# The image sort of a four-stage convolution block: four rounds made one, its turn from columns to lines cut in halves

## What is computed

```python
x = x + dct(_gn(x))                    # L0: keeps two bands of a 56x56 DCT
x = x + similarity(_gn(x), 5x5)        # L1: 5x5 patches weighted by cosine similarity over the channels
x = x + gate(_gn(x))                   # L2: a gate per channel
x = x + attention(_gn(x), ...)         # L3
```

```python
xh = x[:, :16]                                   # the first half of the channels
idx_h = argsort(xh, axis=-2); xs = take(xh, idx_h)   # sort each column
idx_w = argsort(xs, axis=-1); xs = take(xs, idx_w)   # then each line
x = concatenate([xs, x[:, 16:]], axis=1)
qkv = fuse(dw3(q), dw5(q), dw7(q)) of q = conv1x1(x)  # five words q1, k1, q2, k2, v
idx = argsort(v over the 3136 pixels)            # the row sort, which carries the four other words
...                                              # attention on sorted words
# the results go back through the inverse of idx, then of idx_w and idx_h
```

## Time and profile before

| | us |
|---|---|
| median of 3 runs | 14788.44 |
| lowest and highest | 14781.02, 14789.07 |
| profiled execution | 14787.32 |
| its span | 14785.4 |
| VectorE busy in it | 13633.2 |
| from the end of VectorE's last round on images to its first instruction of the row sort | 865.1 |

### The profile page before, as it was taken

How to read it: one execution, slowest core, us unless ns; L and a number is a source line. 1 busy time by engine, 2 the same in 40 slices (tenths; PEclk the granted TensorE clock), 3 DMA queues, 4 the chain that set the end, 5 groups by cost and what they waited for, 6 DMA issues and landing times. The chain is left out here.

```text
span 14785.4 us, 119905 instructions
## 1 busy us (share of the span) xinstructions
PE 6701.6 (45%) x42108; PEld 2746.8 (19%) x42108; DVE 13633.2 (92%) x7545; ACT 7055.5 (48%) x6343; POOL 5873.1 (40%) x3844
## 2 busy tenths in 40 slices
PE   4888825760037327426625714814823014433310
PEld 3444401210012112112111212201211002111100
DVE  4888878999999999999999999999999999989978
ACT  0000023455565665565575565565566555444443
POOL 0000000366666666666666666666666630000000
PEclk9999967885568668768857857956966557666655
DMA  1555532100001001001001000100100011221232
GB/s 46 140 140 145 149 78 68 51 27 12 11 12 45 17 11 41 22 12 36 27 11 36 27 12 30 32 12 26 37 12 12 34 33 50 87 67 54 79 76 66
DMA packets 342572, 696.70 MB, mean 47 GB/s; under 512 B 71005, under 2 KB 275006, under 8 KB 331126
## 3 DMA queue, kind: packets, MB, share of 16 engines
q1 hardware_dynamic: 337398, 673.49, 16.7%
q10 hardware_dynamic: 4544, 15.26, 0.4%
HBM read 479.77 MB, written 208.74 MB: 47 GB/s over the span
## 5 line engine op out<-in xcount | busy, mean ns | idle before, releaser
L1194 DVE COPY_PREDICATED arena<-psum,arena 128x2048 f32<-128x2048 uint32 (+23 forms) x1280 | 3968.9, 3104 | 71.3 <-ACT psum L1154 70.5
L1201 DVE COPY_PREDICATED arena<-psum,arena 128x2048 f32<-128x2048 uint32 (+23 forms) x1280 | 3932.9, 3076 | 42.0
L1020 PE MATMUL psum<-arena,wt 128*32 128x448 f32 x31360 | 3210.1, 571 | 1217.2 <-DMA arena<-xpad 695.1
L1119 POOL TENSOR_TENSOR arena<-arena 128x512 int32<-128x512 int32 (+23 forms) x1280 | 2037.7, 1593 | 3124.3 <-DVE arena L1186 3121.8
L1105 POOL TENSOR_TENSOR arena<-arena 128x512 bf16<-128x512 f32 (+23 forms) x1280 | 1930.8, 1509 | 3031.1 <-SPq L270 2830.8
L1142 ACT ACTIVATE arena<-arena 128x2048 f32<-128x2048 f32 (+23 forms) x1280 | 3032.1, 2371 | 70.4 <-DVE arena L1201 38.1
L1162 ACT ACTIVATE masks<-psum 128x512 fp8e4<-128x512 f32 (+25 forms) x1256 | 917.5, 731 | 3555.5 <-DVE arena L1201 3554.5
L1111 POOL TENSOR_TENSOR arena<-arena 128x512 int32<-128x512 int32 (+23 forms) x1280 | 1960.6, 1533 | 0.0
L1020 PEld LDWEIGHTS psum<-arena,wt 128*32 128x32 f32 x31360 | 1045.5, 114 | 3384.4 <-issue 2311.6
L1410 PE MATMUL psum<-ident,arena 128*112 128x128 f32 x896 | 196.9, 384 | 2432.2 <-ACT arena L1329 1872.9
L1186 DVE TENSOR_TENSOR arena<-arena 128x512 f32<-128x512 f32 (+23 forms) x1280 | 1146.5, 898 | 98.4 <-POOL arena L1111 98.4
(11 more groups left out here) (132 smaller groups left out, 7635.3 us busy)
## 6 DMA issues: line engine op xcount, KB each, us to landing
arena<-xpad SPq DMA_DIRECT2D x896, 108.5 KB, 2.3
arena<-simd SPq DMA_DIRECT2D x416, 210.0 KB, 4.2
arena<-simd SPq DMA_DIRECT2D x416, 196.0 KB, 4.1
xpad<-arena SPq DMA_DIRECT2D x8, 1924.0 KB, 8.1
arena<-in_x SPq DMA_DIRECT2D x8, 1568.0 KB, 7.5
x3d<-arena SPq DMA_DIRECT2D x8, 1568.0 KB, 5.2
prodd<-arena SPq DMA_DIRECT2D x8, 1568.0 KB, 5.2
arena<-prodd SPq DMA_DIRECT2D x8, 1568.0 KB, 14.7
```

Of the source, the lines that this page charges most:

```text
L1020: last = nc.tensor.matmul(psum[C * b:C * b + C, n % C_BANKS, 0:CROWS * W], wt[:, g, C * w:C * w + C], cx[i % 2][b][:, y0:y0 + CROWS, x0:x0 ...
L1119: last = nc.gpsimd.tensor_tensor(hi, packed_view(stmp, here, piece, 1), lo, ALU.subtract)
L1194: last = nc.vector.copy_predicated(lo, wide_mask(q, k, piece, here), hi)
L1201: last = nc.vector.copy_predicated(hi, wide_mask(q, k, piece, here), packed_view(ptmp, here, piece, NP))
```

## The change

All four images are sorted in one round. The two buffers `bk` become four: `bp` and `bq` for the column stages, `br` and `bs` for the line stages. `bx`, `bp`, `bq` and `bs` lie where the words of tile 1 of the row sort will be, `br` and `bin_` above tile 0's, so the convolution can write tile 0 meanwhile.

- **Start.** The load of `bin_` for u = 0 is issued before SP's part of the last `a_` round; that of `bx` stays behind it.
- **Between images.** ScalarE copies `bin_` of image u + 1 into `bp` behind stage 23 of image u (`first`). VectorE goes from stage 41 of one image to stage 0 of the next; ScalarE turns `bs` back into `bx` then.
- **The turn.** Stage 20 is done on columns 0 to 27 and then 28 to 55. ScalarE turns the first half behind the first, the second behind the second. Stage 21 is done on lines 0 to 27 when the first half is there and on lines 28 to 55 when the second is.
- **Loads.** The eight loads of the next image stand one by one behind the mask stores of stages 6 to 13, no longer together behind that of stage 5.
- **Convolution of tile 0.** One pass over all seven chunks through u = 1 to 3. The row sort's first round no longer waits for the last store to `xpad`; ScalarE does so before it writes the words of tile 1 (`stored`), and SP at that round's end.

The diff, of the functions `b_scalar` and `b_vector` only the new text (the old stands above):

```diff
...
         b_in, b_out, b_mst = sem("b_in"), sem("b_out"), [sem(f"b_mst{i}") for i in range(4)]
+        b_first, b_mid = sem("b_first"), sem("b_mid")
         b_cp, b_mk, b_hi, b_xp = sem("b_cp"), sem("b_mk"), sem("b_hi"), sem("b_xp")
 
-        b_sems = [*b_mst, b_cp, b_mk, b_hi, b_xp]
+        b_sems = [*b_mst, b_in, b_first, b_mid, b_cp, b_mk, b_hi, b_xp]
         st = [0]
-        bin_ = take(st, XPN)
         bx = take(st, XPN)
+        bp, bq, bs = (take(st, N) for _ in range(3))
+        assert st[0] <= NWD * N
+        st = [2 * NWD * N]
+        br, bin_ = take(st, N), take(st, XPN)
+        assert st[0] <= B_END
         bini, bxi = (v[:, 0:WP * WP].rearrange("p (h w) -> p h w", w=WP)[:, R3:R3 + H, R3:R3 + W] for v in (bin_, bx))
-        bk = [take(st, N), take(st, N)]
+        HALF = H // 2
         SI = len(IMG_NET)
 
         def turned(v):
             return v.rearrange("p (h w) -> p w h", w=W)
 
-        def b_load(sp, u, dst, loaded):
-            for b in range(UB):
+        def b_load(sp, u, dst, loaded, images=range(UB)):
+            for b in images:
                 sp.dma_start(dst[CS * b:CS * b + CS, :], xpad_u[u, b, 0:CS]).then_inc(loaded, 16)
 
-        def b_begin(sp):
-
-            b_load(sp, 0, bin_, b_in)
-            b_load(sp, 0, bx, b_out)
-
-        def b_sync(sp, u, beside, more):
+        def b_sync(sp, conv):
             count = [0] * 4
-            for d in range(2):
-                for s, (at, _, n) in enumerate(IMG_NET):
-                    q = d * SI + s
+            for u in range(U):
+                for i in range(2 * SI):
+                    d, s = divmod(i, SI)
+                    at, _, n = IMG_NET[s]
+                    q = 2 * SI * u + i
                     sp.wait_ge(b_mk, q + 1)
-                    sp.dma_start(img_masks[2 * u + d, :, at * W:(at + n) * W], masks[:, q % 4, 0:n * W]).then_inc(b_mst[q % 4], 16)
+                    sp.dma_start(img_masks[2 * u + d, :, at * W:(at + n) * W],
+                                 masks[:, q % 4, 0:n * W]).then_inc(b_mst[q % 4], 16)
                     count[q % 4] += 1
-                    if q == 2:
-                        sp.wait_ge(b_out, 16 * UB)
-                    if q % 3 == 2:
-                        next(beside, None)
-                    if q == 5 and more is not None:
-                        sp.wait_ge(b_cp, 1)
-                        sp.sem_clear(b_in)
-                        b_load(sp, more, bin_, b_in)
-            sp.wait_ge(b_xp, 1)
-            sp.sem_clear(b_out)
-            for b in range(UB):
-                sp.dma_start(xpad_u[u, b, 0:CS], bx[CS * b:CS * b + CS, :]).then_inc(b_out, 16)
-            for _ in beside:
+                    if u == 1 and i == 2:
+                        sp.wait_ge(b_out, 16 * UB * 2)
+                    if u and i % 3 == 2:
+                        next(conv, None)
+                    if u + 1 < U and 6 <= i < 6 + UB:
+                        if i == 6:
+                            sp.wait_ge(b_first, u + 1)
+                        b_load(sp, u + 1, bin_, b_in, (i - 6,))
+                sp.wait_ge(b_xp, u + 1)
+                for b in range(UB):
+                    sp.dma_start(xpad_u[u, b, 0:CS], bx[CS * b:CS * b + CS, :]).then_inc(b_out, 16)
+            for _ in conv:
                 pass
             for i in range(4):
                 sp.wait_ge(b_mst[i], 16 * count[i])
-            if more is None:
-                sp.wait_ge(b_out, 16 * UB)
...
+        def b_bufs(d, s):
+            a, b = (bp, bq) if d == 0 else (br, bs)
+            return (a, b) if s % 2 == 0 else (b, a)
+
+        def b_copied(u, d):
+
+            return (2 * SI + 2) * u + (SI + 2) * d
+
+        def b_scalar(act, conv):
+
+            def first(u):
+                act.wait_ge(b_in, 16 * UB * (u + 1))
+                if u:
+                    act.wait_ge(b_hi, 2 * SI * (u - 1) + SI)
+                nc.scalar.activation(img3(bp), bini, ACT.Copy).then_inc(b_first, 1)
+
+            first(0)
+            for u in range(U):
+                for i in range(2 * SI):
+                    d, s = divmod(i, SI)
+                    q = 2 * SI * u + i
+                    if i == SI:
+                        for h in range(2):
+                            if h == 0:
+                                act.wait_ge(b_mid, u + 1)
+                                act.wait_ge(b_cp, b_copied(u, 0) + SI)
+                            else:
+                                act.wait_ge(b_hi, q)
+                            w = slice(HALF * h, HALF * h + HALF)
+                            nc.scalar.activation(img3(br)[:, w, :], turned(bq)[:, w, :], ACT.Copy).then_inc(b_cp, 1)
+                    act.wait_ge(b_cp, b_copied(u, d) + s)
+                    if i == 0:
+                        act.wait_ge(b_first, u + 1)
+                    if q:
                         act.wait_ge(b_hi, q)
+                    src, dst = b_bufs(d, s)
+                    runs = unpaired(IMG_NET[s][1], H)
+                    for lo, hi in runs:
                         ins = nc.scalar.activation(dst[:, W * lo:W * hi], src[:, W * lo:W * hi], ACT.Copy)
                     if runs:
                         ins.then_inc(b_cp, 1)
                     else:
                         act.sem_inc(b_cp, 1)
+                    if u and i % 3 == 2:
+                        next(conv, None)
+                    if i == SI + 2 and u + 1 < U:
+                        first(u + 1)
+                act.wait_ge(b_hi, 2 * SI * (u + 1))
+                act.wait_ge(b_cp, b_copied(u + 1, 0))
+                act.wait_ge(b_out, 16 * UB * (u + 1))
+                nc.scalar.activation(bxi, turned(bs), ACT.Copy).then_inc(b_xp, 1)
+            for _ in conv:
                 pass
 
         def b_vector(dve):
+
+            def exchange(rows, src, dst, mask, part, marked=None):
+                def side(buf, piece, k):
+                    return part(pair_views(buf, piece, W)[k])
+
+                for piece, at in rows:
+                    last = nc.vector.tensor_tensor(part(packed_view(mask, at, piece, W)), side(src, piece, 0),
+                                                   side(src, piece, 1), ALU.is_gt)
+                if marked is not None:
+                    last.then_inc(marked, 1)
+                for op, k in ((ALU.min, 0), (ALU.max, 1)):
+                    for piece, at in rows:
+                        last = nc.vector.tensor_tensor(side(dst, piece, k), side(src, piece, 0), side(src, piece, 1), op)
+                return last
+
+            def columns(h):
+                return lambda v: v[:, :, HALF * h:HALF * h + HALF]
+
+            def lines(h):
+                return lambda v: v[:, HALF // 2 * h:HALF // 2 * h + HALF // 2, :]
+
+            for u in range(U):
+                for i in range(2 * SI):
+                    d, s = divmod(i, SI)
+                    rows = IMG_NET[s][1]
+                    q = 2 * SI * u + i
+                    src, dst = b_bufs(d, s)
+                    mask = masks[:, q % 4, :]
+                    if i == 0:
+                        dve.wait_ge(b_first, u + 1)
+                    if i != SI:
+                        dve.wait_ge(b_cp, b_copied(u, d) + s)
                     if q:
                         dve.wait_ge(b_hi, q)
                     if q >= 4:
                         dve.wait_ge(b_mst[q % 4], 16 * (q // 4))
+                    if i == SI - 1:
+                        assert len(rows) == 1
+                        exchange(rows, src, dst, mask, columns(0)).then_inc(b_mid, 1)
+                        last = exchange(rows, src, dst, mask, columns(1), b_mk)
+                    elif i == SI:
+                        assert len(rows) == 1
+                        if u:
+                            dve.wait_ge(b_xp, u)
+                        dve.wait_ge(b_cp, b_copied(u, 1) - 1)
+                        exchange(rows, src, dst, mask, lines(0))
+                        dve.wait_ge(b_cp, b_copied(u, 1))
+                        last = exchange(rows, src, dst, mask, lines(1), b_mk)
+                    else:
+                        last = exchange(rows, src, dst, mask, lambda v: v, b_mk)
                     last.then_inc(b_hi, 1)
...
-        def c_scalar(act, b, chunks, pace):
+        def c_scalar(act, b, chunks, pace, stored=0):
 
             n = 0
             for _ in range(2 * pace):
                 yield
+            if stored:
+                act.wait_ge(b_out, stored)
...
             close_round(sp, a_sems + a_pre[(T - 1) % 2])
+            b_load(sp, 0, bin_, b_in)
             a_sync(sp, T - 1, None, T % 2, taps=False, more=False)
             close_round(sp, a_sems)
-            b_begin(sp)
-            for u in range(U):
-                b_sync(sp, u, c_sync(sp, 0, C_FIRST[u], 1) if u else iter(()), u + 1 if u + 1 < U else None)
-                close_round(sp, b_sems + (c_sems if u else []))
+            b_load(sp, 0, bx, b_out)
```

(21 more changed lines are left out.)

41 lines of the change are left out of this document (3 added, 38 removed).

## The result

| | before, us | after, us |
|---|---|---|
| median (4 runs each) | 14787.15 | 14678.83 |
| lowest and highest | 14781.02, 14789.07 | 14677.25, 14688.42 |
| profiled execution (span) | 14787.32 (14785.4) | 14688.42 (14686.6) |
| VectorE's stretch: end of the last round on images to the row sort | 865.1 | 763.3 |

The ratio is 0.9929, 95% interval 0.9917 to 0.9941: 0.7% faster. The forecast was 14688, within 14673 to 14718. In five later runs the changed kernel took 14682.96 to 14695.58, median 14691.33, ratio 0.9934 (0.992 to 0.9947). The median of all nine is 14685.6.

The account below looks back on a forecast made before the run. VectorE, busy 92% of the span, was taken to bound the kernel, so its idle time counts. Savings of 17.6 + 54.0 + 18.0 + 7.8 + 3.0 = 100.4 us from 14787.3 gave 14686.9, put at 14688 for the median, range 14673 to 14718.

Parts of the forecast that it names:

- The start: Before image 0: its load, issued one round earlier, lets ScalarE copy as soon as the round closes; 17.6 us saved.
- The boundaries: Between images: no close, VectorE goes straight on, losing 0.8 us per boundary instead of 18.8; 54.0 us saved.
- The turn: Columns to lines in halves, four times: shorter waits for ScalarE, less 2.4 us for 24 added instructions; 18.0 us saved.
- The masks: VectorE's waits for mask stores to land: 14.8 us go, 7 come back behind stores and convolution loads; 7.8 us saved.
- The step from five waits to one cause: The five mask-store waits, 14.8 us, all come from the block of eight image loads behind stage 5.
- The end: Before the row sort: the wait for the last stores' landing moves into the next round; 3.0 us saved.
- The account before: VectorE's work and idle time in the old image sort sum to 865.2 us of the 865.1 us stretch.
- a fifth place: In the old image sort: claimed not to exist, as work plus four kinds of idle time filled the stretch.
- (a): Rival at three boundaries: masks land late behind eight stores, VectorE stands 10 us each, 30 us given back, 14718; chance 0.10.
- (b): Rival: the turn's halves wait as long as the whole, or the early load is late; 18 us lost, 14706; chance 0.10.
- (c): Rival: TensorE at 1.2 GHz takes 21 us a word, delaying ScalarE and VectorE; 187 us slower, 14975; chance 0.04.
- the point named, 12.8: TensorE's time per word, in us, from which (c) decides: ScalarE evicts a word every third stage, 3 x 4.3.

Follow-up runs that it names:

- counted: Changed kernel with ScalarE's stage-0 count of images 1 to 3 given by a one-element copy instead of a bare increment; 14679.46 us (one run), stretch 762.7.
- double_stores: Changed kernel with each image's eight stores issued twice, the first eight to a spare tensor; 14721.55 us (one run), stretch 800.5.
- long_words: Changed kernel with seven extra groups of unused products in each word of tile 0 on TensorE; 14779.23 us (one run), stretch 858.5.

## Why the prediction was right

**The start** was forecast at 17.6 and gave 28.84 - 11.11 = 17.7; undone, 17.5.

**The boundaries** were forecast at 54.0 and gave 56.5 - 0.6 = 55.9. The mechanism was right but for one step, which failed: "VectorE asks for it at 5.4 and waits 0.7": there is no wait at stage 1 of any image. ScalarE's count for a stage in which it copies nothing is a bare increment, and it went out while the turn back was under way (2106.74 against an end at 2112.64); counted shows that the wait is there when the count hangs on an instruction. That the 2.89 us copy for the next image fits behind stage 23 was right: no wait is there.

**The turn** was forecast at 18.0. Its waits fell from 25.7 to 4.2 and the busy time of the two rows grew by 2.7 (2.4 forecast): 18.8; undone, 18.3. The 24 instructions really cost a little less: the waits with a releaser fell from 150.6 to 46.6, by 104.1, and the stretch by 101.8, which leaves 2.2, or 0.09 us each. By the Trainium skill's 150 cycles an instruction ("VectorE: DVE Perf Modes", "The TRN2 errata — SBUF-src ops pay a fixed extra latency per instruction") they would have cost an estimated 3.8; in the stretch they cost between the page's 58 cycles (0.06 us at 0.96 GHz) and its 150 (0.16 us). The durations in the rows show why: two masks of 784 elements take 2 x 0.97 and one of 1568 takes 1.79, 0.15 more for the cut, but an instruction starts some 0.08 us before the one ahead of it has ended (2106.74 + 1.79 = 2108.53 against 2108.45).

**The masks** were forecast at 7.8 and gave 14.8 - 10.1 = 4.7. Here a term was mis-sized. The 6.0 at stage 7 of image 1 were 5.7, but "no wait, or 0.5" at stage 4 was 1.02, 2.10 and 1.22. In image 1 two things of less than 1 us each add up there: VectorE came 0.7 earlier, because of the missing wait at stage 1, and mask 0 landed 4.9 us after its issue, where I had let it follow the last store's landing by 0.7 and so come 4.1 after its issue. In image 2 the turn back (6.50 us) and the eight stores (9.16 us) took longer as well. And the block's cost was taken from before: undone in the new order it costs 17.1, not 14.8, since the convolution's chunks fall on other stages. The step from five waits to one cause was right.

**The end** was forecast at 3.0 and gave 3.6.

**The account before** (865.2 of 865.1) closed by luck. Its 714.6 counts the overlaps of instructions twice, where VectorE was busy for 700.6, and it left out 13.9 us of gaps of some 0.08 us ahead of each stage's mask: the 140.9 in the earlier trace rows less the 127.0 that have a releaser there. So there was a fifth place; the change did not touch it (14.2 us after).

**The sum**: 17.7 + 55.9 + 18.8 + 4.7 + 3.6 = 100.7, with 0.7 of small waits 101.4 (101.9 with 2.2 for the added instructions); the stretch shrank by 101.8, and 100.4 had been forecast. That the forecast lay only 1.4 off is partly luck: the boundaries (1.9), the turn (0.8) and the end (0.6) brought more than forecast, the masks 3.1 less, and this nearly cancelled. The rivals: (a) did not happen and double_stores shows why, (b) did not happen (both parts undone cost what they were said to bring), (c) did not happen, and long_words shows that it would have with words of 15.8 us; the point named, 12.8, was not tested. Its argument that gaps of up to 3.65 us leave a word at 10.73 did not hold throughout: behind gaps of 3.19 and 3.62 us two words took 12.43 and 13.65. ScalarE waited for TensorE just once, for 1.5 us. What the prediction left out is that the rest of the program moves by some 10 us from run to run; its range was wide enough for that.

## What to carry to other kernels

When rounds are merged, lay out the issuing queue of the DMAs anew: a block of stores or loads that cost nothing while everybody waited for the close stands in front of the small stores on which the next stage depends, and it costs nothing until the slack of the ring is used up (here the turn back, 8.7 us of issuing and the mask's landing overran four stages by 1 to 2 us); from there on each microsecond of issuing costs one (9.4 more issued, 9.3 more waited). Drawn apart, the same stores also took less issuing, 0.45 us each in pairs. But drawing such a block apart moves whatever is behind it in the chain, the loads, then the first product, then the eviction, and each of these has its own place in a queue that must move along. Measure an edit of 5 us by the stretch of the trace that it touches, which in the two profiles of the same kernel agreed within 0.3 us, and not by the total, whose medians differed by 12.5.

## What the runs showed of the hardware that I had not expected

- A bare semaphore increment in ScalarE's queue doesn't wait for the activation ahead of it: the stage-0 count was given some 6 us before the turn back ended. Hung on an activation of one element, it came behind it: in counted the turn ran from 2098.39 to 2104.43, the small activation from 2104.34 to 2104.52, and VectorE went on at 2104.55.
- What a store costs SP to issue depends on how many it issued just before. Stores from 16 partitions took 0.9 us for two at a time (0.45 each), but 8.74 us for eight in a row, the first two 0.34 and 0.42 and the others 0.94 to 1.60; sixteen loads to 16 partitions in a row took 7.29 us, 0.45 each. The stores landed 4.6 us after their issue (median), the mask behind eight or sixteen of them 4.7 to 5.2, and a mask behind eight loads 14.7; the median of all masks in the kernel before was 1.8.
- In long_words TensorE never stood still and the granted clock was 1.00 (2.4 GHz) over 500 us; the 112 products of a word took 10.70 us. In the changed kernel, where it stood 0.6 to 6.7 us before most words of images 2 and 3, most words still took 10.73. Two of those shown singly in the timeline took 12.43 and 13.65: the granted clock over them was 0.86 and 0.78, behind idle times of 3.19 and 3.62 us, and 1.00 over a word behind 1.90.
